# Start and expert-weight splits reordered in the first stage of a four-stage transformer kernel

## The reference

```
x = x + xattn0(layernorm(x), token_ids, ctx, ctx, ctx)   # 4 experts picked by token id; Wg = Wu = Wd = ctx
x = x + ffn0(layernorm(x), router, experts, shared)      # 16 experts, top 4, and a shared expert
x = x + xattn1(layernorm(x), ctx, segments, ...)         # 16 heads, latent keys, look-back mask
x = x + ffn1(x, gate, up, down)                          # ternary weights, 8-bit activations
```

## Time and profile before

| | us |
|---|---|
| median of 3 runs | 585.29 (583.1 to 588.38) |
| the profiled execution | 586.61 |
| its span in the profile | 584.8 |
| busy: PE, VectorE, ScalarE, GpSimd | 501.4, 450.2, 356.9, 317.5 |

### The profile page before, as it was taken

How to read it: one execution, slowest core, us unless ns; L and a number is a source line. 1 busy time by engine, 2 the same in 40 slices (tenths; PEclk the granted TensorE clock), 3 DMA queues, 4 the chain that set the end, 5 groups by cost and what they waited for, 6 DMA issues and landing times.

```text
span 584.8 us, 11047 instructions
## 1 busy us (share of the span) xinstructions
PE 501.4 (86%) x3338; PEld 440.6 (75%) x3338; DVE 450.2 (77%) x1358; ACT 356.9 (61%) x903; POOL 317.5 (54%) x298
## 2 busy tenths in 40 slices
PE   0699979998899798986568999999899999588895
PEld 0488768877788797975358999999899998346673
DVE  4679967884878777736688889999989886859774
ACT  2344556342667677642237877878688889656643
POOL 2538661114477886315768788788576772353100
PEclk9989999999999999985587999999999999879997
DMA  7144444312455464469500000100000000000000
GB/s 274 40 122 126 140 149 121 102 45 70 110 191 152 141 185 114 124 200 305 144 14 24 24 24 18 30 18 1 2 1 2 2 1 2 0 1 6 13 28 27
DMA packets 27816, 45.24 MB, mean 77 GB/s; under 512 B 5680, under 2 KB 18832, under 8 KB 27120
## 3 DMA queue, kind: packets, MB, share of 16 engines
q1 hardware_dynamic: 20912, 28.15, 15.5%
q0 software_dynamic: 3792, 10.74, 7.4%
q10 hardware_dynamic: 3056, 5.65, 2.9%
HBM read 34.63 MB, written 8.85 MB: 74 GB/s over the span
## 4 chain that ended last, share of the span: by engine, by line
PE 46%; DVE 25%; issue 9%; DMA 7%; ACT 6%; POOL 4%; SPq 0%; DVEq 0%; ACTq 0%; POOLq 0%
PE bank L1076 8%; PE bank L415 7%; PE bank L416 7%; PE bank L417 7%; PE bank L1517 5%; DMA bw<-bits_dram 3%; DVE pT_lo L1576 2%; DVE sc L2073 1%; PE bank L1472 1%; ACT pr L952 1%; PE bank L1278 1%; DVE X L1628 1%; PE bank L1280 1%; PE bank L1279 1%; DMA slots_y<-yb 1%
## 5 line engine op out<-in xcount | busy, mean ns | idle before, releaser
L578 POOL DMA_INDIRECT inb<-rows_kept,row_of x47 | 47.7, 1014 | 37.8 <-PE bank L1076 20.8
L952 ACT ACTIVATE pr<-sc,smin 128x256 f32<-128x256 f32 x128 | 63.3, 502 | 0.0
L657 POOL TENSOR_TENSOR Q_lo<-Q,Q_hi 128x512 fp32r<-128x512 f32 x32 | 41.5, 1298 | 23.7 <-ACT Q_hi L691 23.2
L2073 DVE CUSTOM_DVE_ANT_0 sc<-bank,bias 128x256 f32<-128x256 f32 x128 | 46.4, 418 | 0.2 <-issue 0.2
L644 POOL TENSOR_TENSOR pr<-pr,srec 128x512 f32<-128x512 f32 x32 | 33.3, 1041 | 21.8 <-DVE srec L2080 21.7
L1576 DVE TENSOR_TENSOR pT_lo<-bank,pT_hi 128x512 fp32r<-128x512 f32 x64 | 41.1, 682 | 4.8 <-ACT pT_hi L691 4.8
L691 ACT ACTIVATE pT_hi<-bank 128x512 fp32r<-128x512 f32 x64 | 35.0, 596 | 13.6 <-PE bank L1076 13.3
L651 POOL TENSOR_TENSOR Q<-Q,rot 128x512 f32<-128x512 f32 x32 | 41.1, 1286 | 2.1 <-DVE Q L2062 2.1
L606 POOL DMA_INDIRECT yk<-slots_y,slot x32 | 33.1, 1033 | 16.1 <-DMA slots_y<-yb 6.1
L1076 PE MATMUL bank<-const,pr 128*128 128x128 f32 x256 | 34.8, 279 | 5.8 <-POOL pr L644 5.7
L961 ACT ACTIVATE pr<-pr,srec 128x256 f32<-128x256 f32 x64 | 29.1, 502 | 16.7 <-DVE srec L2080 16.7
(11 more groups left out here) (346 smaller groups left out, 1942.7 us busy)
## 6 DMA issues: line engine op xcount, KB each, us to landing
slots_y<-yb SPq DMA_DIRECT2D x47, 128.0 KB
wg_raw<-gate_up_dram SPq DMA_DIRECT2D x22, 256.0 KB, 2.7
bw<-bits_dram ACTq DMA_DIRECT2D x3, 1024.0 KB
wd_raw<-down_dram SPq DMA_DIRECT2D x16, 128.0 KB, 2.1
wo<-wo_dram SPq DMA_DIRECT2D x2, 1024.0 KB
wd_raw<-down_dram SPq DMA_DIRECT2D x30, 64.0 KB, 2.3
gu_raw<-gate_up_dram SPq DMA_DIRECT2D x6, 256.0 KB, 3.6
X<-x_dram SPq DMA_DIRECT2D x2, 512.0 KB, 6.6
```

The lines of the kernel that those rows point to most:

```text
L578: pool.indirect_dma_start(inb[:, j % NIN, :], None, rows_d, bass.IndirectOffsetOnAxis(row_of[:, j:j + 1], 0)).then_inc(slots_in[j % NIN], 16)
L657: pool.tensor_tensor(Q_lo[:, i % 2, :], Q[:, i % 2, :], Q_hi[:, i % 2, :].bitcast(F32), ALU.subtract).then_inc(queries_low_g, 1)
L952: e = act.activation(pr[:, i % 2, z, :], sc[:, i % 2, z, :], ACT.Exp, bias=smin[:, i % 2, z:z + 1], scale=-1.0, accum_out=ssum[:, i % 2, z ...
L2073: dve.tensor_tensor_reduce(sc[:, r, z, :], bank[2 + h][:, u * S:(u + 1) * S], bias[:, TB * b_ + u, :], 1.0, 3.0e38, ALU.add, ALU.min, smin ...
```

## The change

The loads of X, context and constants are cut into smaller ones and put in the order of use: X in tiles 0, 1 to 3, 4 to 7; the context in quarters, those of columns z=0 first, one k on SP's and one on ScalarE's queue; of the constants the identity first. A Silu over 8 elements is put ahead of all copies. The context's split goes by quarters, all low parts on VectorE (GpSimd made half of them before). VectorE normalises tile 0 before it makes the masks, and makes the moments of tiles 1 to 3 in step -1, those of tiles 4 to 7 and the tables in step 0. ScalarE's copies of the gate and up chunks move from step i to step i+1 (chunks 2i and 2i+1 in step i); GpSimd's `power` for tiles 4 to 7 moves behind two of its splits. The rest of SP's, GpSimd's and ScalarE's lists stays.

```diff
@@ sync
-            for i in range(2):
-                sp.dma_start(X[:, 4 * i:4 * i + 4, :], x_d[:, 4 * i:4 * i + 4, :]).then_inc(x_in[i], 16)
-                if i == 0:
+            load_x(0, 0, 1)
+            for z in range(2):
+                cols = slice(z * HALF, (z + 1) * HALF)
+                sp.dma_start(ctxT[:, 0, cols], ctxT_d[:, 0, cols]).then_inc(context_in[z], 16)
+                if z == 0:
                     sp.dma_start(tok[:, :], tok_d).then_inc(tokens_in, 16)
-                    sp.dma_start(seg[:, :], seg_d).then_inc(tokens_in, 16)
+            load_x(1, 1, NT // 2)
+            sp.dma_start(seg[:, :], seg_d).then_inc(x_in[2], 16)
+            load_x(2, NT // 2, NT)
@@ gpsimd
             power(0, 0, 1).then_inc(rstd_g, 1)
-            pool.wait_ge(context_high_a, 1)
-            lo(ctx_lo[:, 0, :], ctxT[:, 0, :], ctx_hi[:, 0, :]).then_inc(context_low_g, 1)
             pool.wait_ge(variance_v, 2)
             power(0, 1, NT // 2 - 1).then_inc(rstd_g, 1)
-            pool.wait_ge(variance_v, 3)
-            power(0, NT // 2, NT // 2).then_inc(rstd_g, 1)
...
-            for c in range(8):
+            for c in range(2):
+                lo_expert_gu(c)
+            pool.wait_ge(variance_v, 3)
+            power(0, NT // 2, NT // 2).then_inc(rstd_g, 1)
+            for c in range(2, 8):
                 lo_expert_gu(c)
@@ scalar
-            act.dma_start(const[:, 0:K_COS], const_d[:, 0:K_COS]).then_inc(identity_in, 16)
-            for k in range(KD):
-                act.dma_start(ctxT[:, k, :], ctxT_d[:, k, :]).then_inc(context_in[k], 16)
+            act.dma_start(ident, const_d[:, K_ID:K_ID + P]).then_inc(identity_in, 16)
+            for z in range(2):
+                cols = slice(z * HALF, (z + 1) * HALF)
+                act.dma_start(ctxT[:, 1, cols], ctxT_d[:, 1, cols]).then_inc(context_in[z], 16)
+            act.dma_start(const[:, K_ONE:K_COS], const_d[:, K_ONE:K_COS]).then_inc(x_in[2], 16)
+            act.wait_ge(step_g, 1)
+            act.activation(fo[:, :], mhalf[:, :], ACT.Silu)
...
-            for k in range(KD):
-                act.wait_ge(context_in[k], 16)
-                copy(ctx_hi[:, k, :], ctxT[:, k, :]).then_inc(context_high_a, 1)
+            def hi_context(q):
+                z, k = divmod(q, 2)
+                act.wait_ge(context_in[z], 32)
+                copy(ctx_hi[:, k, z * HALF:(z + 1) * HALF], ctxT[:, k, z * HALF:(z + 1) * HALF]).then_inc(context_high_a, 1)
+            for q in range(KD):
+                hi_context(q)
@@ scalar, loop over i
                     hi1(i + 1)
+                if i == -1:
+                    for q in range(KD, 2 * KD):
+                        hi_context(q)
...
-                for c in (2 * i + 2, 2 * i + 3):
-                    if c < C_MOE:
+                for c in (2 * i, 2 * i + 1):
+                    if 0 <= c < C_MOE:
                         hi_expert_gu(c)
                 if 0 <= i - 3 < NT - 1:
                     hi_expert_dn(i - 3)
@@ tensor
                 for z in range(2):
+                    if t == 0:
+                        pe.wait_ge(context_low_v, KD * (z + 1))
@@ vector
-            dve.wait_ge(tokens_in, 32)
...
+            def expert_masks():
+                dve.wait_ge(tokens_in, 16)
...
+            def tables():
...
+            def lo_context(q):
+                z, k = divmod(q, 2)
+                cols = slice(z * HALF, (z + 1) * HALF)
+                dve.wait_ge(context_high_a, q + 1)
+                lo(ctx_lo[:, k, cols], ctxT[:, k, cols], ctx_hi[:, k, cols]).then_inc(context_low_v, 1)
...
+            lo_context(0)
             norm1(0)
-            for t in range(1, NT // 2):
-                moments(0, t)
...
-            dve.wait_ge(context_high_a, 2)
-            lo(ctx_lo[:, 1, :], ctxT[:, 1, :], ctx_hi[:, 1, :]).then_inc(context_low_v, 1)
+            lo_context(1)
+            expert_masks()
             for i in range(-1, NT + 5):
...
                     lo1(i + 1)
+                if i == -1:
+                    for q in range(KD, 2 * KD):
+                        lo_context(q)
+                    dve.wait_ge(x_in[1], 16)
+                    for t in range(1, NT // 2):
+                        moments(0, t)
+                    dve.tensor_scalar(vare[:, 0, 1:NT // 2], ...).then_inc(variance_v, 1)
...
                     gprod(i)
-                if i == -1:
-                    dve.wait_ge(x_in[1], 16)
+                if i == 0:
+                    dve.wait_ge(x_in[2], 48)
                     for t in range(NT // 2, NT):
                         moments(0, t)
...
+                    tables()
```

More of the change, by code:

```diff
@@ L248, in build @@
             m[k] for k in "lanes hit pt comb lane tileno row_f tile_p".split()]
-        x_in = [sem(f"x_in{i}") for i in range(2)]
+        x_in = [sem(f"x_in{i}") for i in range(3)]
         context_in = [sem(f"context_in{i}") for i in range(KD)]
@@ L266, in build @@
          gated_low_v, experts2_p, x_after1_v, norm_turned_p, norm_high_a, norm_low_v, routed_p, context_high_a,
-         context_low_v, context_low_g, identity_in, step_g, stats_v, router_high_a,
+         context_low_v, identity_in, step_g, stats_v, router_high_a,
          router_low_v, small_in, kv_kept, egu_high_a, egu_low_g, edn_high_a, edn_low_g, edn_low_v) = [sem(n) for n in (
@@ L271, in build @@
              "experts2_p x_after1_v norm_turned_p norm_high_a norm_low_v routed_p context_high_a context_low_v "
-             "context_low_g identity_in step_g stats_v router_high_a router_low_v small_in "
+             "identity_in step_g stats_v router_high_a router_low_v small_in "
              "kv_kept egu_high_a egu_low_g edn_high_a edn_low_g edn_low_v").split()]
@@ L421, in _, with load_x @@
         def _(sp):
-            for i in range(2):
-                sp.dma_start(X[:, 4 * i:4 * i + 4, :], x_d[:, 4 * i:4 * i + 4, :]).then_inc(x_in[i], 16)
-                if i == 0:
+            def load_x(i, a, b):
+                sp.dma_start(X[:, a:b, :], x_d[:, a:b, :]).then_inc(x_in[i], 16)
+            load_x(0, 0, 1)
[3 more added lines that the diff above has]
+                if z == 0:
                     sp.dma_start(tok[:, :], tok_d).then_inc(tokens_in, 16)
-                    sp.dma_start(seg[:, :], seg_d).then_inc(tokens_in, 16)
+            load_x(1, 1, NT // 2)
+            sp.dma_start(seg[:, :], seg_d).then_inc(x_in[2], 16)
+            load_x(2, NT // 2, NT)
             sp.dma_start(rw[:, :, :], router_d[:, :, 0:RC]).then_inc(small_in, 16)
@@ L1186, in _ @@
             for i in range(-1, NT + 5):
[L1187 to L1190, removed]
                 if 0 <= i < NT:
@@ L1607, in _ @@
-            copy(one16[:, :], ones)
+            def expert_masks():
+                dve.wait_ge(tokens_in, 16)
+                for e_ in range(3):
+                    link(dve.tensor_scalar(ge[:, e_, :], tok[:, :], float((e_ + 1) * PER_EXPERT), None, ALU.is_ge))
+                dve.tensor_scalar(pick[:, 0, :], ge[:, 0, :], -1.0, 1.0, ALU.mult, ALU.add)
+                dve.tensor_tensor(pick[:, 1, :], ge[:, 0, :], ge[:, 1, :], ALU.subtract)
+                dve.tensor_tensor(pick[:, 2, :], ge[:, 1, :], ge[:, 2, :], ALU.subtract)
+                copy(pick[:, 3, :], ge[:, 2, :])
@@ new lines, in tables @@
+            def tables():
+                copy(segf[:, 0, :], seg[:, :])
+                link(dve.tensor_scalar(segf[:, 1, :], seg[:, :], float(-LOOKBACK), None, ALU.add))
+                link(dve.tensor_tensor(hn[:, 2, 0:P], ident, keyix[:, 0:P], ALU.mult))
+                link(dve.tensor_reduce(rowix[:, :], hn[:, 2, 0:P], AX_X, ALU.add))
+                dve.tensor_scalar(upper[:, :], rowix[:, :], float(R), None, ALU.is_ge)
+                dve.tensor_scalar(tri[:, :], keyix[:, 0:P], rowix[:, 0:1], None, ALU.is_gt)
+                copy(one16[:, :], ones)
@@ L1719, in lo_dn @@
                 lo(dn_lo[:, c % 2, :], dn_raw[:, c % 2, :], dn_hi[:, c % 2, :]).then_inc(down_low_v, 1)
+            lo_context(0)
             norm1(0)
-            for t in range(1, NT // 2):
-                moments(0, t)
-            dve.tensor_scalar(vare[:, 0, 1:NT // 2], mv[:, 0, 1:NT // 2, 1], EPS, None, ALU.add).then_inc(variance_v, 1)
-            dve.wait_ge(context_high_a, 2)
-            lo(ctx_lo[:, 1, :], ctxT[:, 1, :], ctx_hi[:, 1, :]).then_inc(context_low_v, 1)
+            lo_context(1)
+            expert_masks()
             for i in range(-1, NT + 5):
@@ L1737, in _ @@
                     lo1(i + 1)
+                if i == -1:
[4 more added lines that the diff above has]
+                        moments(0, t)
+                    dve.tensor_scalar(vare[:, 0, 1:NT // 2], mv[:, 0, 1:NT // 2, 1], EPS, None, ALU.add
+                                      ).then_inc(variance_v, 1)
                 sel1(i, 3)
```

## The result

The changed kernel takes **616.57 us** (median of 4 runs, 615.09 to 617.04); the kernel before beside it 584.86. The ratio is 1.051, interval 1.0477 to 1.0543. The profiled execution took 615.09, its span 28.5 us more than before's.

A forecast was written before the change was run, and what follows sets the result against it. PE and VectorE together were taken to bound the eight-tile loop at 6.55 us a step, with GpSimd's queue late at its end. Longer steps (+35.7 us) less head start (6.2) gave +29.5 on 585.3: 615 us, range 606 to 624.

The forecast's parts named there:

- Head start: Kernel start: first product 8.2 us earlier (5.6 to 9.5), of which 6.2 us (3.5 to 8) stay at step 3.
- The gain's cover: Steps 0 and 1: slow-clock product1(0), VectorE's moments (2.8 us) and tables (1.3) cut the gain to 6.4 us at product1(2).
- Second wait: Loop: ScalarE waits for down weights fetched only after the second split; 4.5 us from split to Wd copy, step 11.35 us.
- Which wait ends last: Loop: the down load ends last, setting the step at 11.35 us; the rstd wait alone would give 10.2.
- the other wait: Loop: VectorE's hn waits for GpSimd's power behind the splits, until 5.1 us after the step's first Wg copy.
- Rival (b): Loop: only GpSimd's order bites, as down weights land within 3.4 us of the split; 602 us, chance 8%.
- Steps 8 to 10: Loop's end: 9.3 us without silu, then two steps of 8.9 with H_hi alone, between Wd and the next Wg copy.
- rival (c): PE's clock falls in the new gaps: some 3 us in the loop, 2.4 at the next stage's start; 620 us, 12%.
- The sum: From step 3's first Wg copy (S3) to power(7)'s end: 77.6 us against 41.9, +35.7; less 6.2 head start, +29.5.
- Rival (a): Loop: the later copies are hidden and only the 6.2 us head start stays; 579 us, chance 5%.
- Rival (d): Start: context in only at 7.8 and step 0's new VectorE load eats the rest; head start 1 to 3, 619 us, 8%.
- What I had counted at nothing: Start: further DMA issues push expert loads back some 2 us, and context splits run beside product1(0); both cost nothing.

The follow-up runs named there:

- down copies later: The changed kernel, with ScalarE copying the down weights one step later too (expert i-4 in step i): 611.69 us, ratio 1.0426 to the kernel before.
- splits alone: The kernel before, with only ScalarE's gate and up copies changed to chunks 2i and 2i+1 in step i: 619.32 us, ratio 1.0552.
- start alone: The changed kernel, with ScalarE's gate and up copies back in their old steps: 584.04 us, ratio 0.9958 to the kernel before.
- loop's end reordered: Changed kernel with old chunk-copy steps, plus last two rstd, next stage's first splits earlier and last down copy behind H_hi(6): 581.49 us, ratio 0.9894 to kernel before.
- GpSimd's list moved: The changed kernel, with power(t) ahead of the splits of chunks 6+2t and 7+2t and the down split one place later: 613.48 us, ratio 1.0445.
- tables in step 1: The run with the loop's end reordered, plus VectorE's tables made in step 1 instead of step 0: 579.98 us, ratio 0.9862 to the kernel before.
- down load first: The changed kernel, with the down block's load ahead of the two chunk loads in SP's list: 611.43 us, ratio 1.0408 to the kernel before.

## Why the prediction was right

The forecast was 615 (606 to 624), the measured 616.57.

- **Head start**: 8.2 us at the first product forecast, 8.14 measured; 6.2 at step 3 forecast, 5.94 measured (42.97 against 37.03). Context was in at 5.46, I took 5.2. The estimate of 4.3 from the figures of the Trainium skill, DMA: Bandwidth & Descriptors, section Anatomy of one DMA, was 1.2 us too early; its fit is given for DMAs that GpSimd issues, and these were issued by SP and ScalarE. The bounds from the rows (3.9 and 7.8) held the measured landing. The gain's cover, product1(0) at the lower clock and then VectorE's moved moments and tables, took what I had set for it: product1(2) at 23.34, forecast 22.9.
- **Second wait**: the term of 4.5 us between the end of the second split and the Wd copy was 4.1 (61.57 to 65.71), just under the shortest that the trace of before showed (4.2). That SP and the DMA engines had less else to do may be the reason; no run tests it. From Wd to the next Wg copy it was 3.3 and not 3.54. So the step was 10.65 and not 11.35: 42.5 us for four steps against 45.4.
- **Which wait ends last**: the down load, by some 0.6 us a step. Both edits that make it old show this, and that the other wait then gives 10.0 to 10.1, where I had 10.2. Rival (b) was therefore mispriced: with the down load out of the way the time is about 610 (1.0426 times 585.3), and the 602 that I gave it was too low, because I let its three last steps go at 6.4 us, where they took 9.8, 9.4 and 7.9 in the run with the down copies later. With 610 for (b), the total time alone would hardly have told it from the forecast; the two runs that make the load old do.
- **Steps 8 to 10**: forecast 9.3, 8.9, 8.9, measured 10.1, 10.1, 8.5. There the path went another way than I had it: not over the down load but over GpSimd's rstd, the x1 selections and the product behind them, and ScalarE's H_hi waited for PE (1.2 and 1.8 us). That product ran at the lower clock: its six matmuls took 2.9 us (85.88 to 88.81), where six at 0.23 us apart behind a first of 0.50 would take some 1.65 (an estimate from the rows). That is rival (c), which I gave 12%: it is true in part, and the 2.0 us by which steps 8 and 9 were too long offset two thirds of the 2.9 us that the shorter steps gave back. It also cost 2.4 us at the start of the next stage; both stood in the price of (c) and not in the sum.
- **The sum**: S3 to the end of power(7) 76.2 us against 77.6; with the head start +28.3 against +29.5; with the 2.4 at the next stage's start +30.7. The untouched rest of the profiled execution gave 2.2 back, so its span grew by 28.5. The medians differ by 31.7, since the profiled execution of the kernel before lay 1.8 above its median and this one 1.5 below. So the path and the step were right, but that the total came within 2 us of the forecast is luck in part: the shorter steps (2.9 us), the longer steps 8 and 9 (2.0), the slow start of the next stage (2.4) and the 2.2 of the rest nearly cancelled.
- **Rival (a)** needed the second split to be through GpSimd before hn is due; the run with the splits alone shows 36.9 us of just this wait. **Rival (d)** is out by the 9.04.
- What I had counted at nothing was nothing in the changed kernel: ScalarE's first chunk copy (16.59) waited for no load, and the last two splits of the context (9.27 to 10.56) were done before the second half of product1(0).

One term had the right size for this kernel and the wrong owner: the 6.2 us of head start at step 3, all put down to the start. The first selection of step 3 came at 39.0 before, 36.3 with the splits alone, 34.9 with the start alone and 33.0 with both: 2.7, 4.0 and 6.0 us sooner. So rival (a), priced at the full 6.2, and my 577 to 581 for the start alone were too hopeful. Alone the start was worth 2.5 us (0.5 to 4.4 by its interval), and the traces say where the rest went: it is 8.2 us ahead at the first product and 7.2 at the second, 4.0 at the third (25.31 against 29.32, after the moved moments and tables and the 2.0 us beside GpSimd's splits), still 4.0 at the first gate_up product, 2.5 at the first `hid` (PE's clock), and 1.0 behind the wait for `bsum`. Between the splits alone and the full change the first gate_up product moved 4.3 us (118.9 to 114.6), so the start's worth at that place was about the same with either order of the splits.

## What to carry to other kernels

When one engine's step is moved in kernels whose engines follow lists written by hand, write down for each other list what stands directly behind the moved step's result, small things first: here a 0.5 us rstd and a 0.25 MB load that had no part in the edit made the step 4 us longer. Price each of the waits alone, since with one of them removed the next stands right behind it (0.5 us here), and a test that undoes only one says little of the other. A head start is not time yet: here 8.2 us at the first product were 4.0 two tiles on and 1.0 in the slot stage. Read it again at each later place, and look there for what ends last, also for short operations that now stand beside another engine's long ones and for waits on loads that nobody touched.

## What the runs showed of the hardware

**PE's clock behind idle stretches.** The slot stage has one such place in every run, the wait for `bsum`. Idle stretches of 1.16 to 1.18 us (the changed kernel and three others) and of 1.43 us (before) left the higher level in place. Behind 1.65 us (loop's end reordered), 1.70 (GpSimd's list moved), 2.70 (start alone) and 3.06 us (tables in step 1) came the lower one, and the clock of some 20 us around it was 0.91, 0.91, 0.91 and 0.83 where it was 1.00 before. But the length alone doesn't decide: behind 1.79 us at the same place (down load first) the level held. At the start of the gate_up stage it held behind 1.78 us (before) and fell behind 1.90 (start alone), and after the same 2.44 us one run was at the lower level from the first matmul (down load first) and another only from the third (down copies later). The Trainium skill, TensorE: Matmul & The Clock Gate, Part 1, says that the same kernel spends a different number of its first matmuls at the lower level from one execution to the next, by a phase that the kernel doesn't choose; that would fit these rows, but each is of one profiled execution, and what decides is left open.

**VectorE beside GpSimd.** A split on GpSimd that starts just before a short operation of VectorE holds it up: the first h1n and the tables' last operation took 0.94 and 1.09 us longer with the start alone than in the changed kernel, which is the 2.0 us by which step 1 came later. Selections, which read PSUM, kept their 0.48 us beside such splits. The Trainium skill, SBUF — State Buffer, "Who interferes with whom", says that copies, casts and tensor-scalar operations of VectorE can take a port pair that GpSimd shares, and that the later of the two is blocked; these rows agree for the two that work from SBUF to SBUF.
